# Softmax sums through a fourth work bank, and their reciprocals as exp(-ln) with one Newton step

## The reference

```
h   = group_norm(x, 32 groups) * gn_w + gn_b
q, k, v = qkv_w h + qkv_b                      (8 heads of 32 channels)
a   = softmax(q k^T / sqrt(32)) v              per head, 1024 x 1024
y   = x + proj_w a + proj_b                    end of layer 0
q1, k1, v1 = Wq y, Wk y, Wv y                  (32, 32 and 256 channels)
out = gamma * softmax(q1 k1^T) v1 + y          layer 1, one head
```

## Time and profile before

| | |
|---|---|
| three runs, median (lowest to highest) | 1515.11 us (1514.18 to 1516.34) |
| the profiled execution | span 1513.1 us from the first to the last instruction; no other time is given for it |
| instructions | 20608 |
| TensorE matmul, weight load | 1476.9 us (98%), 892.7 us (59%) |
| VectorE, ScalarE, GpSimd | 1099.3 us (73%), 745.2 us (49%), 1168.3 us (77%) |

### The profile page before, as it was taken

The page is one execution under the profiler, slowest core; times in us unless marked ns, Lnnn a source line. Parts: engine busy times, 40 slices in busy tenths (PEclk is TensorE's granted clock), DMA queues, the critical chain, the costliest instruction groups (busy, mean ns, idle before and its releaser), DMA issues.

```text
span 1513.1 us, 20608 instructions
## 1 busy us (share of the span) xinstructions
PE 1476.9 (98%) x7248; PEld 892.7 (59%) x7248; DVE 1099.3 (73%) x1922; ACT 745.2 (49%) x1373; POOL 1168.3 (77%) x540
## 2 busy tenths in 40 slices
PE   8899999999999999999999999999999999999988
PEld 6454455567555765558555675557655585556547
DVE  4777868787787878877687777878778776775343
ACT  2356446644566355653556445563546536554412
POOL 2278579985899678994899858997789949898704
PEclk8799999999999999999999999999999999999979
DMA  5223132120503014030421205030140303100100
GB/s 150 48 67 78 36 74 60 38 48 31 139 22 85 15 48 113 17 85 22 106 64 30 56 22 147 23 84 15 44 112 22 85 21 98 44 1 8 49 21 29
DMA packets 47143, 85.24 MB, mean 56 GB/s; under 512 B 11072, under 2 KB 21184, under 8 KB 47040
## 3 DMA queue, kind: packets, MB, share of 16 engines
q1 hardware_dynamic: 46896, 83.74, 22.0%
q10 hardware_dynamic: 144, 0.20, 0.1%
HBM read 18.29 MB, written 8.39 MB: 18 GB/s over the span
## 4 chain that ended last, share of the span: by engine, by line
PE 82%; DVE 8%; ACT 4%; SPq 2%; issue 2%; DMA 1%; POOL 0%; ACTq 0%; DVEq 0%; POOLq 0%
PE pv L596 15%; PE pv L574 15%; PE st L565 14%; PE work L651 13%; PE work L714 7%; DVE mpart L954 6%; PE work L673 3%; PE work L721 3%; PE work L685 3%; ACT probs L789 2%; PE st L557 2%; SPq L396 2%; PE rec L615 2%; PE work L659 2%; PE work L679 1%
## 5 line engine op out<-in xcount | busy, mean ns | idle before, releaser
L925 POOL TENSOR_TENSOR acc<-acc,probs 128x1024 f32<-128x1024 f32 x372 | 871.0, 2380 | 19.8 <-ACT probs L789 18.9
L789 ACT ACTIVATE probs<-st 128x512 f32<-128x512 f32 x1152 | 610.6, 602 | 422.1 <-PE st L565 201.2
L954 DVE TENSOR_REDUCE mpart<-work 128x1 f32<-128x512 f32 x1008 | 636.1, 678 | 136.3 <-PE work L651 133.8
L651 PE MATMUL work<-ks,qs 96*128 96x512 f32 x1008 | 430.5, 469 | 9.2 <-DMA ks<-part_hi 2.4
L565 PE MATMUL st<-qs,ks 98*128 98x512 f32 x1024 | 395.7, 429 | 7.0 <-DMA qs<-mrow 3.1
L925 POOL TENSOR_TENSOR acc<-probs 128x1024 f32<-128x1024 f32 x64 | 151.1, 2373 | 191.4 <-ACT probs L789 191.3
L651 PEld LDWEIGHTS work<-ks,qs 96*128 96x128 f32 x1008 | 190.6, 193 | 143.2 <-DVE mpart L954 68.0
L565 PEld LDWEIGHTS st<-qs,ks 98*128 98x128 f32 x1024 | 193.3, 191 | 119.1 <-ACT probs L789 65.3
L596 PE MATMUL pv<-probs,l_vt 128*128 128x256 f32 x1024 | 240.8, 381 | 0.7 <-ACT xa L862 0.5
L574 PE MATMUL pv<-probs,vt 128*32 128x512 f32 x2048 | 236.3, 602 | 0.0
L596 PEld LDWEIGHTS pv<-probs,l_vt 128*128 128x128 f32 x1024 | 193.8, 191 | 35.8 <-ACT probs L789 5.9
(11 more groups left out here) (82 smaller groups left out, 953.4 us busy)
## 6 DMA issues: line engine op xcount, KB each, us to landing
qs<-part_hi SPq DMA_DIRECT2D x120, 128.0 KB, 2.4
ks<-part_hi SPq DMA_DIRECT2D x120, 128.0 KB, 2.4
xa<-in_x SPq DMA_DIRECT2D x16, 512.0 KB, 4.4
y<-in_x SPq DMA_DIRECT2D x8, 1024.0 KB, 6.1
out<-xa SPq DMA_DIRECT2D x32, 256.0 KB, 2.2
qs<-part_lo SPq DMA_DIRECT2D x60, 128.0 KB, 2.4
ks<-part_lo SPq DMA_DIRECT2D x60, 128.0 KB, 2.4
l_qs<-part_hi SPq DMA_DIRECT2D x32, 64.0 KB, 2.0
```

The source lines that it names most:

```text
L651: last = mm(bank, qs[g][0:HI_HI_LO, c, j, tb * P:(tb + 1) * P], ks[g][0:HI_HI_LO, j, half * HALF:(half + 1) * HALF], start=True, stop=True)
L789: nc.scalar.activation(probs[:, n % PRING, half * HALF:(half + 1) * HALF], st[:, (2 * n + half) % ST_BANKS, :], ACT.Exp).then_inc(s_exp1 i ...
L925: pool.tensor_tensor(a, first, probs[:, n % PRING, :], ALU.add).then_inc(s_add0, 1)
L954: last = dve.reduce_max(mpart[:, 4 * j + tb, half:half + 1], bank, AX.X)
```

## The change

The matmuls of a sum go to a bank of `work`, which has four banks now, as an entry among the others. ScalarE uses it: the logarithm into the SBUF tile `guess`, a copy into the SBUF tile `rec`, then the exponential of minus `guess` in place, which approximates 1/sum. The copy frees the bank. VectorE refines it in two steps, e = rec * guess and rec = (e - 2) * guess, which is minus the reciprocal, and forms the quotient with a factor of -1; in layer 1 one operation scales 512 columns in place, and the last one subtracts. The wait for the quotient before stands ahead of ScalarE's logarithm. ScalarE loads one table set at the start by name. The tables of stops are new for all entries (those of the sums are shown).

```diff
@@ -29,12 +29,11 @@
 PRING = 9
-ST_BANKS, WORK_BANKS = 3, 3
+ST_BANKS, WORK_BANKS = 3, 4
 
 
 L1_AT = 48
-PIECES, PIECES1 = 4, 2
-PIECE = HALF // PIECES
+SUM_STEPS = 3
 
@@ -43,57 +42,57 @@
...
 STEADY = {
...
-    "sums": (10, 14, 14, 16, 23, 72, 74, 75, 100, 118, 134, 135, 135, 141, 146, 153, 154, 154, 154, 157),
-    "sums1": (159, 159, 159, 162, 164, 164, 170, 171, 175, 175, 193, 193),
...
+    "sums": (10, 13, 14, 23, 73, 77, 77, 124, 134, 135, 144, 147, 154, 156, 156, 161),
+    "sums1": (160, 163, 165, 167, 168, 171, 172, 172, 172, 175, 176, 177, 177, 183, 192, 197),
...
 FIRST = {
...
-    "sums": (63, 72, 95, 97, 108, 112, 122, 151, 155, 157, 162, 166, 185, 203, 206),
...
+    "sums": (64, 70, 73, 103, 113, 116, 119, 158, 163, 166, 172, 202),
...
 LAST = {
...
-    "sums": (9, 11, 26, 30, 32, 56, 57, 67, 111, 122, 143, 152, 155, 155, 156, 163, 165, 166, 167, 167),
-    "sums1": (159, 160, 163, 169, 170, 170, 171, 174, 174, 174, 175, 175),
...
+    "sums": (9, 12, 13, 32, 54, 59, 60, 121, 142, 145, 146, 150, 152, 158, 158, 160),
+    "sums1": (159, 162, 163, 167, 170, 170, 170, 173, 173, 175, 182, 183, 184, 186, 188, 189),
...
 EPILOGUE = {
-    "sums": (3, 3, 6, 6, 10),
...
-    "sums1": (157, 157, 157, 164, 167, 167, 169, 170, 171, 172, 175, 179),
+    "sums": (2, 2, 6, 6),
...
+    "sums1": (157, 160, 162, 163, 163, 166, 167, 169, 169, 171, 172, 173, 173, 173, 185, 185),
...
@@ -113,10 +112,10 @@
     def sums(g, c):
-        return [("SUM", g, c)] + [("R", g, c, p) for p in range(PIECES)]
+        return [("SUM", g, c)] + [("R", g, c, p) for p in range(SUM_STEPS)]
 
     def sums1(c):
-        return [("SUM1", c)] + [("R1", c, p) for p in range(PIECES1)]
+        return [("SUM1", c)] + [("R1", c, p) for p in range(SUM_STEPS)]
 
@@ -152,8 +151,9 @@
 
-NO_BANK = ("SUM", "SUM1", "MC", "MC1", "BN", "AGG", "H", "R", "R1")
-SCALAR_USES = ("VT", "VT1")
+NO_BANK = ("MC", "MC1", "BN", "AGG", "H", "R", "R1")
+SCALAR_USES = ("VT", "VT1", "SUM", "SUM1")
+SUMS = ("SUM", "SUM1")
 
@@ -220,6 +220,8 @@
         acc1 = [acc[:, 1, k, :] for k in range(2)]
+        rec = sb("rec", [P, HALF])
+        guess = sb("guess", [P, HALF])
 
@@ -240,7 +242,6 @@
         pv = ctx.enter_context(nc.psum_tensor("pv", [P, HALF], F32))
-        rec = ctx.enter_context(nc.psum_tensor("rec", [P, HALF], F32))
 
@@ -277,10 +278,11 @@
         s_add1 = sem("s_add1")
-        s_sum = sem("s_sum")
-        s_rec = sem("s_rec")
+        s_ln = sem("s_ln")
+        s_guess = sem("s_guess")
+        s_error = sem("s_error")
+        s_newton = sem("s_newton")
         s_quot = sem("s_quot")
-        s_rec1 = sem("s_rec1")
         s_sc1 = sem("s_sc1")
@@ -307,7 +309,7 @@
 
-            eng.wait_ge(s_sum, sum_no(e, kind, b) + 1)
+            eng.wait_ge(s_w, w_base(kind, b) + place[kind][e] + 1)
 
@@ -602,31 +604,29 @@
 
-            def fill_rec(e, kind, b):
-
-                wait_rec_free(pe, e, kind, b)
...
+            def sum_rows(e, bank, kind, b):
+
+                if e[0] == "SUM1":
+                    pe.wait_ge(s_add1, ADDS1 * (b - 1) + 3 * (e[1] + 1))
+                    return mm(bank[:, 0:QUARTER], ones[:, :], acc1[e[1] % 2][:, 0:QUARTER], start=True, stop=True)
...
-                last.then_inc(s_sum, 1)
+                return last
@@ -684,6 +684,8 @@
                                       start=(k == 0), stop=(k == KT - 1))
+                elif what in ("SUM", "SUM1"):
+                    last = sum_rows(e, bank, kind, b)
                 elif what == "PB":
@@ -726,14 +728,11 @@
                     stops = [[e for e in plans[kind][STOPS * n + k] if e[0] not in NO_BANK] for k in range(STOPS)]
-                    ready = [e for k in range(STOPS) for e in plans[kind][STOPS * n + k] if e[0] in ("SUM", "SUM1")]
                     for half in range(2):
                         if n in units:
                             scores_by_key(n, half, kind, b)
                         for e in stops[half]:
                             fill_bank(e, kind, b)
-                    for e in ready:
-                        fill_rec(e, kind, b)
                     if L1_AT + 2 <= n < L1_AT + 2 + L1_UNITS and n - 2 in units:
@@ -806,6 +805,8 @@
                     act.wait_ge(s_stack[1], 16 * STACK_DMAS * min(b + 1, B))
+                elif e[0] in SUMS:
+                    wait_rec_free(act, e, kind, b)
                 act.wait_ge(s_w, w_base(kind, b) + i + 1)
@@ -826,6 +827,13 @@
                     return
+                elif e[0] in SUMS:
+                    cols = slice(0, HALF if e[0] == "SUM" else QUARTER)
+                    nc.scalar.activation(guess[:, cols], bank[:, cols], ACT.Ln).then_inc(s_ln, 1)
+                    nc.scalar.copy(rec[:, cols], bank[:, cols]).then_inc(s_wa, 1)
+                    act.wait_ge(s_ln, sum_no(e, kind, b) + 1)
+                    nc.scalar.activation(guess[:, cols], guess[:, cols], ACT.Exp, scale=-1.0).then_inc(s_guess, 1)
+                    return
                 else:
@@ -871,6 +879,7 @@
 
+            act.preload_act_table_set("natural_log_exp_and_others")
             act.wait_ge(s_norm_const, 16 * 4)
@@ -913,7 +922,7 @@
                         if ci == 0 and kind != "first":
-                            pool.wait_ge(s_sum, sum_no(sums[kind][0], kind, b))
+                            wait_summed(pool, ("SUM", 1, 0), "first" if b == 1 else "steady", b - 1)
                         elif ci == 1 and kind != "first":
@@ -1033,35 +1042,34 @@
             def own_step(e, kind, b):
-                if e[0] == "R":
-                    _, g, c, p = e
-                    n = chunk_no(e, b)
-                    if p == 0:
-                        wait_summed(dve, ("SUM", g, c), kind, b)
-                    r = rec[:, p * PIECE:(p + 1) * PIECE]
-                    dve.reciprocal(r, r).then_inc(s_rec, 1)
-                    if p == PIECES - 1:
-                        dve.wait_ge(s_rec, PIECES * (n + 1))
-                        dve.wait_ge(s_copy0, n + 1)
+                if e[0] in ("R", "R1"):
+                    owner = ("SUM",) + e[1:-1] if e[0] == "R" else ("SUM1", e[1])
+                    no = sum_no(owner, kind, b)
+                    cols = slice(0, HALF if e[0] == "R" else QUARTER)
+                    r, r0 = rec[:, cols], guess[:, cols]
+                    if e[-1] == 0:
+                        wait_used(dve, owner, kind, b)
+                        dve.wait_ge(s_guess, no + 1)
+                        dve.tensor_tensor(r, r, r0, ALU.mult).then_inc(s_error, 1)
+                    elif e[-1] == 1:
+                        dve.wait_ge(s_error, no + 1)
+                        dve.scalar_tensor_tensor(r, r, 2.0, r0, ALU.subtract, ALU.mult).then_inc(s_newton, 1)
+                    elif e[0] == "R":
+                        _, g, c, _ = e
+                        dve.wait_ge(s_newton, no + 1)
+                        dve.wait_ge(s_copy0, chunk_no(e, b) + 1)
                         a = attn[:, g, c * HALF:(c + 1) * HALF]
-                        dve.tensor_tensor(a, a, rec[:, :], ALU.mult).then_inc(s_quot, 1)
-                elif e[0] == "R1":
-                    _, c, p = e
-                    n = 4 * (b - 1) + c
-                    if p == 0:
-                        wait_summed(dve, ("SUM1", c), kind, b)
-                    r = rec[:, p * PIECE:(p + 1) * PIECE]
-                    dve.reciprocal(r, r).then_inc(s_rec1, 1)
-                    if p == PIECES1 - 1:
-                        dve.wait_ge(s_rec1, PIECES1 * (n + 1))
+                        dve.scalar_tensor_tensor(a, a, -1.0, r, ALU.mult, ALU.mult).then_inc(s_quot, 1)
+                    else:
+                        n = 4 * (b - 1) + e[1]
+                        dve.wait_ge(s_newton, no + 1)
                         dve.wait_ge(s_copy1, n + 1)
-
-                        for m in (1, 0):
-                            dve.scalar_tensor_tensor(rec[:, m * QUARTER:(m + 1) * QUARTER], raw1(c)[:, m, :], gam[:, 0:1],
-                                                     rec[:, 0:QUARTER], ALU.mult, ALU.mult).then_inc(s_sc1, 1)
-                            dve.wait_ge(s_sc1, 2 * n + 2 - m)
-                        dve.tensor_tensor(raw1(c), rec[:, :].rearrange("p (m t) -> p m t", m=KT),
-                                          y[:, :, c * QUARTER:(c + 1) * QUARTER], ALU.add).then_inc(s_quot, 1)
+                        raw = raw1(e[1])
+                        dve.scalar_tensor_tensor(raw, raw, gam[:, 0:1], r.unsqueeze(1).to_broadcast([P, KT, QUARTER]),
+                                                 ALU.mult, ALU.mult).then_inc(s_sc1, 1)
+                        dve.wait_ge(s_sc1, n + 1)
+                        dve.tensor_tensor(raw, y[:, :, e[1] * QUARTER:(e[1] + 1) * QUARTER], raw,
+                                          ALU.subtract).then_inc(s_quot, 1)
                 elif e[0] == "BN":
@@ -1079,6 +1087,8 @@
 
+                    if kind == "first" and (g, c) == (0, 1):
```

(10 more changed lines are left out.)

67 lines of the change are left out of this document (29 added, 38 removed), and 40 rows, old and new, of tables (EPILOGUE, FIRST, LAST, STEADY).

## The result

The changed kernel took 1683.5 us (median of 4 runs, 1678.2 to 1690.6), the kernel before on the same chip 1514.7 us (4 runs): a ratio of 1.112 with a 95% interval of 1.109 to 1.115. It is slower by 11%, where 1498 us, faster by 1.1%, had been forecast, and it lies far above the range's upper end of 1550 us. The profiled execution took 1681.1 us, its span is 1678.9 us, 165.8 us more than before.

A forecast was written before the change was run, and what follows sets the result against it. TensorE, busy 98% of the span, was taken to run at VectorE's pace for stretches; -25 (VectorE), -10 (fourth bank), +18 (ScalarE) on 1513.1, plus 2, gave 1498 us; range 1458 to 1511, to 1550 with rival 1.

The forecast's parts named there:

- The step that failed: VectorE's 224 new operations, both inputs in SBUF, were costed at the old forms' lengths: 70 us layer 0, 76 layer 1.
- Rival 1: VectorE's 224 new operations each wait for GpSimd's running add, mean 0.88 us, 196 us in all: 1545 us; chance 0.33.
- one whole GpSimd instruction more each, 2.38 us: Upper bound on the extra length of each of VectorE's 224 new operations with both inputs in SBUF.
- The share of 0.24: Part of VectorE's time taken to reach the end: 275 of 1008 + 128 maxima's products waited for VectorE.
- VectorE's relief, -25 us: VectorE sheds 250.3 us of reciprocals and following operations, gains 146; 0.24 of the 104 us relief reaches the end.
- The fourth bank, -10 us: One more work bank to reduce during each of 64 pieces of 32 products: 40 us, times 0.24.
- ScalarE, +18 us: ScalarE's logarithm, copy and exponential per sum add 88 us, of which 0.20 reaches the end.
- the share of 0.20: Part of ScalarE's added time taken to reach the end: 230 weight loads waited for one of 1152 exponentials.
- the sum of -17 us: Forecast's net change: -25 for VectorE, -10 for the fourth work bank, +18 for ScalarE.
- Banks held longer, up to 8 us: Sums hold a work bank about 1.2 us where a reduction needs 0.68; 8 us back, put into the range.
- Rival 2: ScalarE's logarithm waits for the quotient before it, 57 us in its queue, cancelling the gain: 1517 us; chance 0.13.
- Rival 3: ScalarE reloads its tables twice a sum for logarithm and exponential, 164 us by 0.20 is 33: 1531 us; chance 0.04.

The follow-up runs named there:

- pool_writes2: Changed kernel with each GpSimd add replaced by three memsets that read nothing, about 2.35 us a set, sums of exponentials left out: 1504.2 us.
- The small programs: Separate programs, no part of the attention: GpSimd runs rows of adds or memsets, VectorE starts an operation among them; a two-SBUF product took 2.81 us beside adds.
- drained: Changed kernel with each large GpSimd add in layer 0 waiting for the end of the add right before it: 1568.7 us, ratio 1.036.
- rec_psum: Changed kernel's order with rec back in PSUM, so three work banks, and no large operation with two SBUF inputs: 1626.4 us, ratio 1.074.
- four_direct: Changed kernel, four work banks, exponential written back into the sum's own bank and read there, no copy or Newton step: 1553.3 us, ratio 1.027.
- lnexp_direct: Kernel before with three work banks; ScalarE makes the reciprocal as exp(-ln) straight in PSUM, no copy or Newton step: 1521.1 us, ratio 1.005.
- lnexp_psum: Kernel before with three work banks; reciprocals replaced by ScalarE's logarithm and exponential and a Newton step on rec in PSUM: 1522.4 us, ratio 1.006.
- quot_sbuf: Kernel before with layer 0's reciprocals sent to an SBUF tile, so only its 32 quotients read two SBUF inputs: 1644.3 us, ratio 1.087.
- no_newton: Changed kernel without the Newton steps and ScalarE's copy, leaving 96 operations with two SBUF inputs: 1671.9 us, ratio 1.106.

## Why the prediction was wrong, step by step

**The step that failed** is the one that costed the new operations: "I take no extra, since the nearest rows (L1047 and L1063, one input in SBUF and one in PSUM) stand at 0.69". The nearest rows differed in just the property that decides. 146 us were forecast, 375 measured, and 139 in pool_writes2, where GpSimd does not read. The count of instructions and their undisturbed lengths were right: 989.9 us for VectorE there, near 995 foreseen.

**Rival 1 was the mechanism,** with the right place and the right sign, and the Trainium skill, SBUF — State Buffer, "Who interferes with whom", had stated it: a VectorE instruction with two SBUF inputs and a GpSimd instruction that reads SBUF shut each other out for a whole instruction. The small programs agree (2.81 us against 0.69, and 0.69 against memsets); in the full kernels VectorE stood through up to six adds, which goes beyond a whole instruction. The rival deserved more than 0.33. Its price was 1545 us, and 1683 were measured, for two reasons.
- The wait per operation was taken as at most one add, mean 0.88 us, 196 us in all. The mean came near, by luck: 375 - 139 = 236 us, 1.05 each. But 18 operations hold 159 - 18 x 0.69 = 147 us of it, in single waits of up to 12 us, and the other 206 have 89 us, 0.43 each, half of what was priced. The bound "one whole GpSimd instruction more each, 2.38 us" was no bound.
- The share of 0.24 by which VectorE's time reaches the end was a count of waits under 0.8 us, not a share of time. 236 us of standing cost 179 us, 0.76. In the stop shown above TensorE was idle for 8.2 of the 9 us from 272 to 281: a pause that long empties the banks, stops ScalarE and then GpSimd, and little of it is hidden. In drained, where no operation is passed over, 271 - 139 = 132 us of standing cost some 22 us by the estimate above, 0.17.

**VectorE's relief, -25 us:** worth next to nothing on the old order (waits of 90 against 95 us with 97 us less work, and 1 us for the next 67). The likely reason, not tested, is that a wait for VectorE comes from what lies ahead of a reduction at that moment and not from VectorE's total.

**The fourth bank, -10 us, and ScalarE, +18 us:** neither was measured alone. ScalarE's 58 us more on the old order, with VectorE's relief, came to 8 us slower; by the share of 0.20 it was to be 12. Its three operations have the forecast lengths at 512 columns (0.60, 0.59, 0.65), and 0.40, 0.39 and 0.45 instead of 0.32 at 256. The bank's worth can only be read with its order: the whole change without the exclusion is 11 us faster than before (1504.2, ratio 0.993), without the bank 112 us slower (rec_psum). So the sum of -17 us was near to what was left once the failed step is taken out, in part by luck, as on the old order the relief's 25 us were not there to be had.

**Banks held longer, up to 8 us:** no run takes this alone. four_direct, which holds the bank until the quotient, is 1553 - 1504 = 49 us slower than pool_writes2. It also differs in that its GpSimd adds where that of pool_writes2 only writes, so the 49 us are not shown to be the bank's.

**Rival 2** is present and small: ScalarE's logarithm waits 30.5 us in seven times for layer 1's last operation, since that stands too; pool_writes2 has no such wait in its list. **Rival 3** fell: one table load, 1283 ns, as before. **The clock** was a follower: 0.933 on average against 0.978, and 0.973 in pool_writes2, with the same instructions and no pauses.

No version that computes the result beats the kernel before. The nearest are lnexp_direct, which leaves the Newton step out, slower by 0.5%, and lnexp_psum, slower by 0.6%.

## What to carry to other kernels

Before moving an operand from PSUM to SBUF, ask whether VectorE's instruction then has two SBUF inputs and whether GpSimd reads SBUF in long rows at that time; the time of the instruction in the old form says nothing of the new one. A saving taken from an average share of waits must not be set against a cost that comes in single blocks: a stop longer than the buffers last is paid almost in full (0.76 over all of them here). If the two engines must meet, let GpSimd wait for its own last instruction between large ones; it cost 0.18 us an add here and gave back 115 of 169 us. The kernel was still slower than before, by 3.6%.

## What the runs showed of the hardware

- A VectorE instruction shut out by GpSimd is not always let in at the end of the running add: 2 to 6 ends of adds passed while it stood (18 of 224, up to 12.35 us). All 53 such operations of the changed kernel, quot_sbuf and no_newton ended 0.55 us after an add that was followed by a gap of 0.08 us or more, and stood through 169 borders without one. With each add waiting for the one before, a gap of 0.14 us, it never happened (0 of 224, 0 of 96, 0 of 32).
- A product of SBUF with a scalar (TENSOR_SCALAR, one input, SBUF to SBUF) was shut out as well: 2.54 us beside the adds, which took 14.00 us instead of 13.82; its length alone stands in no run. A reciprocal of the same size was not (3.35 us, adds at 13.82), nor a reduction (0.69).
- When VectorE gets in between, GpSimd's next add lasts 2.8 us instead of 2.4 (2.83 in the changed kernel's trace), since it now waits in turn.
